# Eight instead of four products per group into an unread PSUM bank, in an attention over sources on one Trainium2 core

## What is computed

```
feat = concatenate([x[src], edge_weights, x[dst]], axis=1)
h = relu(feat @ W_att1.T + b_att1)
scores = (h @ W_att2.T + b_att2)[:, 0]
m = segment_max(scores, src, num_segments=num_nodes)
e = exp(scores - m[src])
denom = segment_sum(e, src, num_segments=num_nodes)
alpha = e / denom[src]
msg = segment_sum(alpha[:, None] * lin_x[dst], src, num_segments=num_nodes)
```

## Time and profile before

| | |
|---|---|
| median of 3 runs | 26595.03 us (26588.95 to 26601.55) |
| profiled execution, its own time | 26592.22 us |
| its span in the profile | 26590.5 us |
| TensorE matmul busy | 19464.4 us (73%) |
| VectorE busy | 16052.1 us (60%) |
| GpSimd busy | 16506.8 us (62%) |
| mean granted TensorE clock | 0.595 |

### The profile page before, as it was taken

One profiled execution on the slowest core, in us unless ns is written; L12 is line 12 of the kernel. 1 busy time (PEld: TensorE's weight loads), 2 busy tenths in 40 slices (PEclk: granted clock), 3 DMA queues, 4 the chain that ended last, 5 costly groups with the idle time before them and its releaser, 6 DMA issues. The chain is left out here.

```text
span 26590.5 us, 540850 instructions
## 1 busy us (share of the span) xinstructions
PE 19464.4 (73%) x107861; PEld 12610.8 (47%) x107889; DVE 16052.1 (60%) x58888; ACT 7043.9 (26%) x24344; POOL 16506.8 (62%) x17229
## 2 busy tenths in 40 slices
PE   5688888888888599999999677777777653333334
PEld 2344444444444355555556355555555433333332
DVE  7788888888888544444445566666666553333333
ACT  0233333333333122222222133333333211111111
POOL 0377777777777377777776255555555437777772
PEclk9555555555555555555555588888888755555555
DMA  7122222222225233333334466666666712222233
GB/s 289 28 44 43 43 44 43 44 43 43 44 43 43 40 76 76 76 76 76 76 76 64 52 110 110 108 109 108 109 111 109 89 30 60 60 60 60 60 56 21
DMA packets 2877529, 1894.36 MB, mean 71 GB/s; under 512 B 2008316, under 2 KB 2481378, under 8 KB 2869682
## 3 DMA queue, kind: packets, MB, share of 16 engines
q0 software_dynamic: 607024, 854.80, 19.9%
q1 hardware_dynamic: 2269906, 1034.48, 18.9%
HBM read 1573.79 MB, written 342.46 MB: 72 GB/s over the span
## 5 line engine op out<-in xcount | busy, mean ns | idle before, releaser
L1262 POOL DMA_INDIRECT H<-tab,a_rs x3520 | 3369.6, 957 | 2970.8 <-issue 2257.1
L850 POOL DMA_INDIRECT H<-tab,idx x3520 | 3387.3, 962 | 2050.0 <-issue 1062.5
L1621 POOL DMA_INDIRECT H<-tab,m_idx x3520 | 3346.6, 951 | 1668.4 <-issue 1022.1
L1793 POOL DMA_INDIRECT g_G<-tab,g_rs x3520 | 3331.7, 946 | 1619.4 <-issue 1059.2
L1545 POOL DMA_INDIRECT rec<-PT,posi x3125 | 3059.1, 979 | 1281.2 <-issue 1026.0
L1855 PE MATMUL g_ps_a<-g_zr,g_oh 128*128 128x64 f32 x7040 | 1712.6, 425 | 2872.7 <-issue 2048.6
L1855 PEld LDWEIGHTS g_ps_a<-g_zr,g_oh 128*128 128x128 f32 x7040 | 1567.5, 328 | 3018.2 <-issue 2240.5
L928 DVE CUSTOM_DVE_ANT_0 junk<-ps_lb,pen 128x512 bf16<-128x512 f32 x3520 | 2292.0, 689 | 845.2 <-PE ps_lb L1035 799.4
L1721 PEld LDWEIGHTS m_ps_a<-m_Sx,H 128*128 128x128 f32 x7040 | 1567.4, 328 | 1414.7 <-issue 1414.0
L1367 PE MATMUL a_ps_z<-a_w_ea,a_eaT 64*128 64x288 f32 x3520 | 1202.6, 466 | 1404.5 <-DVE a_z L1285 1388.3
L1067 PEld LDWEIGHTS ps_a<-V,H 128*128 128x128 f32 x7040 | 1567.2, 328 | 767.3 <-issue 767.3
(11 more groups left out here) (331 smaller groups left out, 40145.5 us busy)
## 6 DMA issues: line engine op xcount, KB each, us to landing
a_rs<-rec SPq DMA_DIRECT2D x880, 164.0 KB, 5.8
g_rs<-rec SPq DMA_DIRECT2D x880, 164.0 KB
rec<-H SPq DMA_DIRECT2D x46, 3116.0 KB
m_row<-key SPq DMA_DIRECT2D x880, 128.0 KB
H<-startp SPq DMA_DIRECT2D x880, 128.0 KB
a_row<-keyc SPq DMA_DIRECT2D x880, 128.0 KB
PT<-in_ea SPq DMA_DIRECT2D x625, 160.0 KB
H<-tab,idx POOLq DMA_INDIRECT x3520
```

The lines of the kernel that those rows point to most:

```text
L850: pool.indirect_dma_start(G[:, k, t, :], None, table, bass.IndirectOffsetOnAxis(ap=idx[:, k, t, :], axis=0)).then_inc(s_g[k], 16)
L1262: pool.indirect_dma_start(G[:, k % SLOTS, t, 0:R], None, tab2, bass.IndirectOffsetOnAxis(ap=rs[:, k, t, 1:2], axis=0)).then_inc(s_g[k % SL ...
L1621: pool.indirect_dma_start(G[:, k, t, :], None, tab1, bass.IndirectOffsetOnAxis(ap=idx[:, k, t, :], axis=0)).then_inc(s_g[k], 16)
L1793: pool.indirect_dma_start(G[:, k, t, :], None, tab3, bass.IndirectOffsetOnAxis(ap=rs[:, k, t, 1:2], axis=0)).then_inc(s_g[k], 16)
```

## The change

`keep_busy(1)` becomes `keep_busy(2)` at all four places of TensorE's loop body. Nothing else in the kernel changes.

```
--- before.py
+++ after.py
@@ -1406,15 +1406,15 @@
                                 pe.matmul(ps_w[:], identb[:], PT[:, 0, 0:3, :].rearrange("p s c -> p (s c)"), start=True, stop=True)
 
                         def body(*at):
-                            keep_busy(1)
+                            keep_busy(2)
                             stage(feature_rows, -1, NG, *at, unroll=U)
                             stage(turn, -2, NG, *at, unroll=U)
-                            keep_busy(1)
+                            keep_busy(2)
                             stage(spread, 0, NG, *at, unroll=U)
                             stage(key_rows, -1, NG, *at, unroll=U)
-                            keep_busy(1)
+                            keep_busy(2)
                             stage(edge_maxima, 0, NG, *at, unroll=U)
-                            keep_busy(1)
+                            keep_busy(2)
                             stage(node_sums, 1, NG, *at, unroll=U)
```

## The result

The changed kernel takes 26688.16 us (median of 6 runs, 26667.65 to 26720.12) against 26591.99 us (6 runs) before: 96 us more, a ratio of 1.0037 with a 95% interval of 1.0024 to 1.005. The forecast was 26715 us. The interval leaves out 1, so the slowdown is clear of the noise. Its profiled execution has a span of 26665.9 us, 75.4 us more than the earlier trace rows.

What follows compares the result with a forecast made beforehand. VectorE and TensorE taking turns, or in some passes the gathers, were taken to bound the stretch; 165 us of longer passes less 45 us of clock gain made +120 us, 26715 us, range 26615 to 26845 us.

Steps and rivals of the forecast that it cites:

- Which places are on the path: At the higher clock, 0.18 us ahead of `edge_maxima` counts fully; `feature_rows` and `spread` add 0; `node_sums` delays only sums.
- the hole before `key_rows`: TensorE gap between `spread` and `key_rows` at the higher clock, claimed to take the 0.18 us of the product ahead of `spread`.
- the gathers only: Ahead of `node_sums`: sums 0.36 us late with the place before; GpSimd's gather, then a later `a_z`, would be late.
- The first group of a pass: Group after each loop start, at the lower clock: no hole in the array, 0.36 to 0.72 us longer, taken as 0.55.
- 165 us less 45: Longer passes, 1.5 us each, cost 165 us; fewer short stretches of low clock give back 45 us: +120 us.
- the slack in the waits for the gather: Waits of `a_z` for gathers, 2.1 us a pass, that could absorb part of the longer groups.
- 199 us: All 110 passes if VectorE and TensorE set the pace throughout: 1.81 us a pass; gathers setting it gave 139 us.
- short drops: Brief low-clock stretches away from the loop's start, some 2 us a pass, worth 59 us if all vanish, taken as 45.
- the 0.27: Cost in us of each microsecond at the lower clock, from first and second group: (7.15 - 5.24)/7.15.
- The clock hardly came back sooner: Rival: denser work restores the clock at once after the loop's start, first group 5.24 us, 210 us back, 26505 us; chance 0.07.
- the stop: VectorE's unnamed 8.10 us wait at each pass's start, read as a reload after its loop branch; expected to stay 8.1 us.
- TensorE's loop brought no fetches: Rival: TensorE's longer loop must be loaded again each pass, at most 2 us overhang, 220 us more; chance 0.01.

Runs made afterwards that it cites:

- the slow series: Four kernels, each doubling one product, against the kernel before at 35008.44 us: `edge_maxima` 1.0023, `feature_rows` 0.9993, `spread` 1.0017, `node_sums` 1.0026.
- the moved loop: The kernel before with 96 empty instructions ahead of VectorE's loop: 25608.81 us against 26604.04 us, 0.9628.

## Why the prediction was right

*Price of a product.* 0.18 us at the higher and 0.36 us at the lower level, as read from two starts, is what the pairs show (0.36 and 0.72).

*Which places are on the path.* Ahead of `edge_maxima` the whole 0.18 is; it alone gave 59 of the 96 us. Ahead of the spread the hole before `key_rows` takes it at the higher clock, and at the lower it costs its 0.36 us in the first group. Ahead of `feature_rows` the ratio was 0.9993 with 1 inside its interval. Ahead of `node_sums` I had let it reach the gathers only. In the slow series it cost 0.26% by way of a wait of `a_dd` that is not explained, and in a series of the usual speed it was not run alone, so what this place adds to the result is not shown.

*The first group of a pass.* I took 0.55 us between 0.36 and 0.72; the pass shown has 7.88 - 7.15 = 0.73, the upper bound, since the clock rose at 17041.3, behind `edge_maxima` at 17039.95. Over all passes the mean grew by 0.51 us: the 0.55 was right, with earlier rises in other passes.

*Sum and clock.* 165 us less 45 was forecast as +120; the profile has +79, the medians +96. The term that was too small is the slack in the waits for the gather. With VectorE and TensorE setting the pace throughout the forecast had 199 us, less 45 for the clock: 154. The traces have 161 from `a_z` to `a_dd`, where the clock's gain is already in. But from 199 to 165 us the forecast left the gathers only 34 us to absorb, and between `a_dd` and the next `a_z` 84 us were absorbed. 7 us too little for the path and 50 us too little for the slack make the 41 us or so by which the forecast lies above the profile. The medians, at +96, come nearer to it than the profile, and that is luck. The clock was about right: I had taken some 2 us of short drops a pass and it was 284/110 = 2.6, of which 1.6 went, 171 us in all; at the 0.27 of the earlier trace rows that is 46 us, against 45. The 0.27 has a second witness in the moved loop, whose first groups lie mostly at the higher clock: (7.15 - 5.16)/7.15 = 0.28. How much of the 161 us the clock gave back was not measured alone.

*What the next profile would show.* One sign of being wrong was that the waits for the gather shrink by as much as the groups grow. They fell by 93 us where the way from `a_z` to `a_dd` grew by 161: not as much, but more than half, and more than the 79 us that are left. The granted clock of 0.89 is a little above the 0.87 or 0.88 named, and there are 7048 products instead of 7044.

*The rivals.* The clock hardly came back sooner behind the stop: the low stretch is 13.6 us before and after in the passes shown, and 1287 and 1246 us in sum. TensorE's loop brought no fetches: over the whole phase the changed kernel has 550 again, and the wait ahead of a pass is 8.03 us.

```profile
q14 instruction: 550, 4.51, 0.2%
```

That the stop is a reload behind VectorE's loop branch was inferred in the prediction from a wait without a name and a count of fetches. The moved loop shows that it depends on where the instructions lie; both went away together. The Trainium skill, "Runtime: NRT & Kernel Launch", section "Instruction fetch mechanics", says that a taken branch to a page no longer loaded stalls the engine until it is fetched; by that rule the traces agree, 550 fetches over the stretch with the stop and 12 over the one without it.

## What to carry to other kernels

In this kernel, products that only keep TensorE's clock up were worth their price while they raised it much (the first four a group), and each further one lengthened the path by its full time where TensorE comes without a hole into a step that another engine waits for. What the kernel then loses is less, if the next limit has slack to absorb it. Put them where TensorE waits anyway, and look for the next limit (here the gather buffers) before counting a shorter path as a gain. If an engine stands still at the start of every pass of an unrolled loop and the instruction queue is fetching then, try to move the loop before tuning anything inside it: 96 empty instructions were worth ten times what this change cost.

## What I had not expected of the hardware

The place of a loop in the instruction memory decided 9.0 us a pass, 3.7% of the kernel; two offsets, 96 and 192 instructions, both did away with it, the second in a single run. And one series ran the same kernel in 35008 instead of 26600 us, with waits in the groups that the profiles of the other series don't have; four of the comparisons had to be read within that series alone. Its cause stays open.
